# Groups of 8 samples by 64 d instead of 128 samples by 4 d: x stored straight from the gathered rows, and the sums over d taken inside a group

## What is computed

```python
e = stack([tbl_f[ids[:, f]] for f in range(32)], axis=1)        # B x 32 x 64
hidden = x = e
for i, (w, b) in enumerate([(w0, b0), (w1, b1)]):
    z = einsum('bhd,bfd->bhfd', hidden, x).reshape(B, -1, D)
    y = relu(einsum('bcd,oc->bod', z, w) + b[None, :, None])     # 128 channels o
    if i == 0: hidden, direct = y[:, :64], y[:, 64:]
    else:      direct = y
    finals.append(direct)
h = concatenate([concatenate(finals, 1).sum(-1), dense_ctx], 1)  # sum over d
h = relu(h @ W_top1 + b_top1); h = relu(h @ W_top2 + b_top2); y = h @ W_top3
```

## Time and profile before

| | us |
|---|---|
| three runs, median (lowest, highest) | 1093.7 (1091.5, 1093.88) |
| the profiled execution | 1092.62 |
| its span, first to last instruction | 1090.8 |
| TensorE busy | 1025.0 (94%) |
| VectorE busy | 944.4 (87%) |
| GpSimd busy | 915.5 (84%) |
| ScalarE busy | 734.9 (67%) |

### The profile page before, as it was taken

The page is one execution under the profiler, slowest core; times in us unless marked ns, Lnnn a source line. Parts: engine busy times, 40 slices in busy tenths (PEclk is TensorE's granted clock), DMA queues, the critical chain, the costliest instruction groups (busy, mean ns, idle before and its releaser), DMA issues.

```text
span 1090.8 us, 10701 instructions
## 1 busy us (share of the span) xinstructions
PE 1025.0 (94%) x3493; PEld 651.4 (60%) x3493; DVE 944.4 (87%) x623; ACT 734.9 (67%) x907; POOL 915.5 (84%) x300
## 2 busy tenths in 40 slices
PE   2059999999999999999999999999999999999999
PEld 1025556656666666666666666666666666666664
DVE  4059999999999999999999999999998989888982
ACT  1036666767777677777777777777777777777761
POOL 7526878779999999999999899997989888988890
PEclk9569999999999999999999999999999999999999
DMA  4278777687878787778877878787777877786730
GB/s 137 55 188 200 194 186 184 180 198 190 210 178 205 183 213 187 192 191 199 207 185 192 201 181 208 182 206 194 194 184 194 204 183 187 191 208 184 183 84 1
DMA packets 142074, 196.89 MB, mean 180 GB/s; under 512 B 15858, under 2 KB 57458, under 8 KB 141891
## 3 DMA queue, kind: packets, MB, share of 16 engines
q1 hardware_dynamic: 137922, 192.01, 70.3%
q0 software_dynamic: 4096, 4.20, 1.8%
HBM read 175.18 MB, written 20.97 MB: 180 GB/s over the span
## 4 chain that ended last, share of the span: by engine, by line
PE 86%; DVE 4%; issue 4%; DMA 3%; ACT 2%; SPq 1%; DVEq 0%; ACTq 0%
PE py L610 40%; PE py L626 15%; PE py L616 14%; PE py L617 14%; DVE zf L498 2%; ACT zh L362 2%; PE py L631 1%; DMA xs<-x_dram 1%; DMA x_dram<-xf 1%; DMA xs<-in_L_rec_w 1%; PE pt L592 1%; DVE zl L515 1%; PE py L675 0%; PE pzS L675 0%; DVE zf L459 0%
## 5 line engine op out<-in xcount | busy, mean ns | idle before, releaser
L303 POOL TENSOR_TENSOR zl<-zf,zh 128x2048 fp32r<-128x2048 f32 x168 | 772.3, 4610 | 116.2 <-ACT zh L362 114.2
L498 DVE TENSOR_TENSOR zf<-xs,hid 128x2048 f32<-128x2048 f32 x256 | 583.3, 2283 | 67.1 <-ACT hid L377 51.9
L610 PE MATMUL py<-zf,wf 128*128 128x512 f32 x1072 | 485.2, 596 | 6.5 <-DVE zf L498 6.5
L362 ACT ACTIVATE zh<-zf 128x2048 fp32r<-128x2048 f32 x186 | 354.9, 1908 | 44.5 <-DVE zf L498 41.1
L610 PEld LDWEIGHTS py<-zf,wf 128*128 128x128 f32 x1072 | 203.5, 190 | 214.2 <-issue 194.2
L616 PE MATMUL py<-zh,wh 128*128 128x512 f32 x744 | 293.6, 395 | 8.7 <-ACT zh L362 8.7
L617 PE MATMUL py<-zh,wl 128*128 128x512 f32 x744 | 292.1, 393 | 0.0
L626 PE MATMUL py<-zl,wh 128*128 128x512 f32 x744 | 233.8, 436 | 0.0
L498 DVE TENSOR_TENSOR zf<-xs,px 128x2048 f32<-128x2048 f32 x64 | 146.4, 2288 | 37.8 <-DMA xs<-x_dram 35.9
L626 PEld LDWEIGHTS py<-zl,wh 128*128 128x128 f32 x744 | 135.9, 189 | 59.2 <-issue 29.2
L293 POOL DMA_INDIRECT emb<-in_tbl,idx x128 | 143.1, 1118 | 29.9 <-issue 24.5
(11 more groups left out here) (71 smaller groups left out, 439.8 us busy)
## 6 DMA issues: line engine op xcount, KB each, us to landing
xs<-x_dram SPq DMA_DIRECT2D x640, 256.0 KB
x_dram<-xf SPq DMA_DIRECT2D x64, 320.0 KB
emb<-in_tbl,idx POOLq DMA_INDIRECT x128
xs<-in_L_rec_w SPq DMA_DIRECT2D x2, 512.0 KB
xs<-in_L_rec_w SPq DMA_DIRECT2D x1, 1024.0 KB
wt<-in_W_top SPq DMA_DIRECT2D x1, 512.0 KB
wt1b<-in_W_top SPq DMA_DIRECT2D x1, 256.0 KB
wt1a<-in_W_top SPq DMA_DIRECT2D x1, 128.0 KB
```

The lines of the kernel that those rows point to most:

```text
L303: pool.tensor_tensor(zl[:, q], zf[:, s], zh[:, q].bitcast(F32), ALU.subtract).then_inc(lo["P"], 1)
L362: act.activation(zh[:, q], zf[:, s], ACT.Copy).then_inc(hi, 1)
L498: dve.tensor_tensor(zf[:, slot(u)], left, right, ALU.mult).then_inc(mult, 1)
L610: mm = pe.matmul(y, wf[:, w, h], zf[:, s, h], start=first and h == 0, stop=ends and h == T - 1)
```

## The change

A group becomes NS = 8 samples by all 64 d. Then a gathered row (one sample, one field, 64 d, 256 B) is already a piece of a row of x, and:

- `stage_x`, `turn_x`, `copy_xf`, the tiles `stage`, `xf`, `pt` and their waits go. SyncE stores x straight from `emb`, in batches of fields as they are gathered (`store_batch`), in pieces of 256 B, five copies as before. `x_dram` is laid out by chunk, so a group's rows are 2048 B pieces at a step of 32 KB. Loads have the sizes they had.
- Chunk 0 is gathered and stored in batches of 12, 12, 6 and 2 fields. Later chunks go 3 or 2 fields a period, stored one period after the gather, in the same place of SyncE's order where `store_x` stood. `emb` holds two chunks instead of four; GpSimd waits for a chunk's stores before it gathers over it.
- A group holds whole sums over d: `add_1`, `add_2` and `sum_d` are replaced by one TENSOR_REDUCE a layer and group out of PSUM, 512 elements to 8 results (`sum_1`, `sum_2`).
- `py1` gets a second PSUM bank (the one of `pt`), so P(g+1) no longer waits for the readers of P(g), but for those of P(g-1). `sum_1(g)` stands behind the products of P(g+1) and its tail, not ahead of them.
- In the beginning xd(1) is loaded ahead of x0(1), xt(1) and xe(0).

```diff
-            def store_x(k):
-                sp.wait_ge(xf_ready, k + 1)
-                dst = x_dram[k, 0:1, :]
-                sp.dma_start(bass.AP(tensor=dst.tensor, offset=dst.offset, ap=[[N, F], [P, ND], [F * N, REPEATS], [1, P]]),
-                             view(xf, 0, [[0, REPEATS], [1, P]])).then_inc(x_stored, 16)
+            def store_batch(n):
+                c, f, m = BATCHES[n]
+                sp.wait_ge(gathered[n % BATCH_SEMS], gathered_count(n))
+                if m < REPEATS:
+                    for i in range(m):
+                        dst = x_dram[c, f + i:f + i + 1, :]
+                        sp.dma_start(bass.AP(tensor=dst.tensor, offset=dst.offset, ap=[[D, P], [F * P * D, REPEATS], [1, D]]),
+                                     view(emb, (c % 2 * F + f + i) * D, [[0, REPEATS], [1, D]])).then_inc(x_stored[c], 16)
+                else:
+                    for i in range(REPEATS):
+                        dst = x_dram[c, i * F + f:i * F + f + 1, :]
+                        sp.dma_start(bass.AP(tensor=dst.tensor, offset=dst.offset, ap=[[D, P], [P * D, m], [1, D]]),
+                                     emb[:, c % 2, f:f + m, :]).then_inc(x_stored[c], 16)
...
-                if g + 3 < G:
-                    store_x(g + 3)
+                if g >= 1 and batch_of(g - 1) is not None:
+                    store_batch(batch_of(g - 1))
...
+                if i == 0 and c >= 2:
+                    pool.wait_ge(x_stored[c - 2], 16 * STORES[c - 2])
+                if i == 0 and n >= BATCH_SEMS:
+                    pool.wait_ge(gathered[n % BATCH_SEMS], gathered_count(n - BATCH_SEMS))
...
                 high(("C", g))
                 if g >= 1:
                     finish_2(g - 1)
-                if g + 3 < G:
-                    copy_xf(g + 3)
                 high(("B", g))
...
+            def sum_1(k):
+                dve.wait_ge(dir1_ready, k + 1)
+                dve.tensor_reduce(zd[H:P, NS * k:NS * k + NS], py1[H:P, k % 2].rearrange("p (b d) -> p b d", d=D),
+                                  AX_X, ALU.add).then_inc(sum1_done, 1)
...
-                add_1(g)
                 if g + 1 < G:
                     products(("P", g + 1))
                     products_s(g + 1)
+                sum_1(g)
...
-                if name == "P" and g >= 1:
-                    pe.wait_ge(swapped, 3 * g)
-                    pe.wait_ge(acc1_done, g)
+                if name == "P" and g >= 2:
+                    pe.wait_ge(swapped, 3 * (g - 1))
+                    pe.wait_ge(sum1_done, g - 1)
...
-                if g + 3 < G:
-                    turn_x(g + 3)
```

More of the change, by code:

```diff
@@ L17 @@
 NC = B // P
[L18 to L21, removed]
+NS = 8
+N = NS * D
+G = B // NS
+GC = P // NS
 T = 4
@@ L47, in mode, with gathered_count, batch_of @@
     return "P"
[L52 to L57, removed]
+FIRST_BATCHES = [(0, 0, 12), (0, 12, 12), (0, 24, 6), (0, 30, 2)]
+PER_PERIOD = [[3] * 10 + [2], [2] * 16, [2] * 16]
+LATER_BATCHES = [(c, sum(PER_PERIOD[c - 1][:i]), n) for c in range(1, NC) for i, n in enumerate(PER_PERIOD[c - 1])]
+BATCHES = FIRST_BATCHES + LATER_BATCHES
+BATCH_SEMS = 4
+STORES = [sum(min(m, REPEATS) for b, _, m in BATCHES if b == c) for c in range(NC)]
+def gathered_count(n):
+    return 16 * sum(BATCHES[i][2] for i in range(n % BATCH_SEMS, n + 1, BATCH_SEMS))
+def batch_of(g):
+    return len(FIRST_BATCHES) + g if g < len(LATER_BATCHES) else None
 def period(g):
@@ L166, in dlrm_tower @@
         px0 = ps("px0", [P, N])
-        pt = ps("pt", [P, N])
         pzS = ps("pzS", [P, N])
[L169 to L174, removed]
+        banks = [py1[:, 0], py2[:, 0], py2[:, 1], hid[:, 0], hid[:, 1]]
+        top1 = [hid[:, 0], hid[:, 1], px0[:], py1[:, 0]]
+        top2 = [pzS[:], py1[:, 1]]
+        x_dram = nc.dram_tensor("x_dram", [NC, REPEATS * F, P * D], F32, kind="Internal")
         ids_in, consts_in, cin_in, top_in = sem("ids_in"), sem("consts_in"), sem("cin_in"), sem("top_in")
-        gathered = [sem("gathered%d" % c) for c in range(NC)]
+        gathered = [sem("gathered%d" % i) for i in range(BATCH_SEMS)]
+        x_stored = [sem("x_stored%d" % c) for c in range(NC)]
         cleared, w_doubled, w_turned = sem("cleared"), sem("w_doubled"), sem("w_turned")
         w_high, w_low, s_low, dense_turned = sem("w_high"), sem("w_low"), sem("s_low"), sem("dense_turned")
-        staged, turned, xf_ready, x_stored = sem("staged"), sem("turned"), sem("xf_ready"), sem("x_stored")
         x0_in, xt_in, xe_in = sem("x0_in"), sem("xt_in"), sem("xe_in")
@@ L261, in load_xe @@
                     sp.dma_start(xe[F * j:F * j + F], block_rows(k, j, T)).then_inc(xe_in, 16)
+            for n in range(len(FIRST_BATCHES)):
+                store_batch(n)
             sp.wait_ge(w_turned, 6)
-            store_x(0)
             load_x0(0)
@@ L290, in _, with gather @@
             pool.wait_ge(ids_in, 16)
-            def gather(c, f):
+            def gather(n, i):
+                c, first, m = BATCHES[n]
+                if i >= m:
+                    return
+                f = first + i
+                if i == 0 and c >= 2:
+                    pool.wait_ge(x_stored[c - 2], 16 * STORES[c - 2])
+                if i == 0 and n >= BATCH_SEMS:
+                    pool.wait_ge(gathered[n % BATCH_SEMS], gathered_count(n - BATCH_SEMS))
                 pool.indirect_dma_start(
-                    out=emb[:, f, c, :], out_offset=None, in_=tables[f],
+                    out=emb[:, c % 2, f, :], out_offset=None, in_=tables[f],
                     in_offset=bass.IndirectOffsetOnAxis(ap=idx[:, c, f:f + 1], axis=0),
-                ).then_inc(gathered[c], 16)
+                ).then_inc(gathered[n % BATCH_SEMS], 16)
             def low(u):
@@ L303, in low @@
                 pool.tensor_tensor(zl[:, q], zf[:, s], zh[:, q].bitcast(F32), ALU.subtract).then_inc(lo["P"], 1)
-            for f in range(F):
-                gather(0, f)
+            for n, (_, _, m) in enumerate(FIRST_BATCHES):
+                for i in range(m):
+                    gather(n, i)
             for g in range(G):
-                now = gathers(g)
+                n = batch_of(g)
                 low(("A", g))
-                for c, f in now[0:1]:
-                    gather(c, f)
+                if n is not None:
+                    gather(n, 0)
                 low(("C", g))
-                for c, f in now[1:2]:
-                    gather(c, f)
+                if n is not None:
+                    gather(n, 1)
                 low(("B", g))
-                for c, f in now[2:3]:
-                    gather(c, f)
+                if n is not None:
+                    gather(n, 2)
         @block.scalar
@@ L560, in _ @@
                 if g >= 1:
-                    add_2(g - 1)
+                    sum_2(g - 1)
                 low(("C", g))
                 products(("D", g))
[L565 to L571, removed]
+            sum_2(LAST)
         @block.tensor
@@ L586, in _ @@
             tr.then_inc(dense_turned, 1)
[L588 to L592, removed]
             def bank(u):
-                return py1[:] if u[0] == "P" else py2[:, u[1] % 2]
+                return (py1 if u[0] == "P" else py2)[:, u[1] % 2]
             def main(u):
@@ L630, in tail @@
                 pe.wait_ge(s_lo, k + 1)
-                pe.matmul(py1[:], wS[:], zS[:], start=False, stop=True).then_inc(y1_ready, 1)
+                pe.matmul(py1[:, k % 2], wS[:], zS[:], start=False, stop=True).then_inc(y1_ready, 1)
             def top_1_begin(m):
@@ L641, in _ @@
             pe.wait_ge(w_low, 3)
-            turn_x(0)
-            turn_x(1)
-            turn_x(2)
             main(("P", 0))
```

109 lines of the change are left out of this document (31 added, 78 removed).

## The result

The changed kernel takes 1102.4 us (median of 14 runs, 1097.5 to 1109.2) against 1093.7: the ratio is 1.009, with a 95% interval of 1.0073 to 1.0107. I had forecast 1085.5 and a range of 1079 to 1096. It became slower. The rival that names the cause (rival 4, the loads come in slower) had been given 0.05.

A forecast was written before the change was run, and what follows sets the result against it. TensorE, busy 94% of the span, was taken as the limit. Span 1090.8 less 7.3 (transposes), 3.8 (copy wait), 1.8 (chunk borders), plus 5.3 (later start) gave 1083.2, hence 1085.5 us forecast; range 1079 to 1096.

The forecast's parts named there:

- rival 4: Loads of 2048 B at a 32 KB step come in slower, DMA full at about 25% more; 1095 us and more; chance 0.05.
- the DMA queues take their new work hidden: Three fields a period cost 2.6 us of stores against 1.16; with 3.7 us of 16.2 free, 1.5 more is hidden.
- the one for rival 4: Sign of slower loads: growing waits of ScalarE for x0, or of VectorE for xd and xe.
- Transposes: 61 TensorE transposes in the periods go, 0.12 us each: 7.3 us gained.
- The high part of B behind the transposed copy: Periods 1, 3, 5, 7, 9: without ScalarE's copy it starts 2 us earlier, saving 0.78 us five times: 3.8 us.
- The chunk borders: VectorE's `sum_d` goes; 0.92 us lost at each of two borders is regained: 1.8 us.
- The reductions: On VectorE 127 additions become 127 PSUM reductions at 0.70 us each, costing nothing since VectorE stays under TensorE.
- Rival 1: Reductions take 1.06 us whatever they read, so VectorE would bound periods 0 to 42; 1088 to 1090 us; chance 0.12.
- The small stores: Twice as many DMA pieces of 256 B, taken at 22 ns each, bounds 19 and 29.
- Rival 2: Small stores are slow, a 256 B packet costing more than a 512 B one; 1104 to 1115 us at 40 ns; chance 0.13.
- The beginning as a whole: Storing chunk 0 delays the first load to about 56.5 us, 5.3 later; then 8.1 to P(0), 15.1 more to A(0).
- The sum: All terms together: 1090.8 - 7.3 - 3.8 - 1.8 + 5.3 = 1083.2 us of span.

The follow-up runs named there:

- the run with 36 KB: The changed kernel with each row of x_dram 4 KB longer, so rows lie at a step of 36 KB instead of 32 KB: 1082.9 us, ratio 0.9908.

## Why the prediction was wrong

**The step that failed** is the sentence that the DMA queues take their new work hidden ("DMA is 0.77 busy, so 3.7 us of 16.2 are free"), together with rival 4's "DMA would go from 0.77 to full at about 25% more; below that nothing". Both weigh throughput, and the sum has no term for how late a load lands. DMA never was full: from 100 to 300 us 0.83 in the changed kernel and 0.87 in the faster one with 36 KB, from 300 to 600 us 0.83 in both. What counted was how late one load lands, in a circle of waits. In the stretch from P(12) to P(44) x0's mean way went from 5.5 to 7.4 us, and the period came out at 15.81 instead of 15.36. Against the run with 36 KB that is 14.5 us there, and 6.4 more from P(0) to P(12): the loss of some 20 us. Of the signs that I had named, the one for rival 4 came (waits of ScalarE for x0 that grow, 24.6 to 209.3 us); its mechanism, DMA near full, did not.

The circle was in the trace of before. ScalarE's copy already waited for x0 there, 21 times in the periods. By the turns of the changed kernel and 0.3 us for `stage_x`, the mean turn of before is about 8.8 + 5.5 = 14.3 us of 15.47, an estimate: 1.2 us of slack, less than the 1.8 us that x0 then became later. I saw the wait on x0 while reading and set it aside, since TensorE was idle nowhere.

What lengthened x0's way was the new layout. I wrote "Loads have the sizes they had" and went on as if they had the time they had. The median went from 5.5 to 6.6 us with the step alone and to 7.0 and over with the stores beside it. The nearest rule is in the Trainium skill, DMA: Bandwidth & Descriptors, section Latency and other measured facts: for copies of 16 KiB a partition it gives 207 GB/s at a row pitch of 512 KiB, 164 at 2 MiB and 103 at 4 MiB, and nothing below 512 KiB. It would have let 32 KB pass. Here 32 KB is slow (1101.5 to 1105.3 us), while 64 and 128 KB are not (1083.6 and 1082.8).

**The steps that held.** The others, read in the run with 36 KB where nothing else is named, since no late load covers them there:
- Transposes: a period of 15.36 where it was 15.47, 0.12 each.
- The high part of B behind the transposed copy: early pairs at 31.42, forecast 31.4, before 32.40.
- The chunk borders: from P(12) on no pair in that run is longer than 30.72.
- The reductions: 0.695 and 0.684 us, forecast 0.70. Rival 1 falls. In the changed kernel itself:

```profile
L526 DVE TENSOR_REDUCE zsum<-py 128x8 f32<-128x512 f32 x64 | 44.1, 689 | 38.1 <-ACT py L404 37.9
...
L521 DVE TENSOR_REDUCE zd<-py 64x8 f32<-64x512 f32 x64 | 44.5, 695 | 2.0
```

- The small stores: in the beginning a piece of 256 B takes a mean of 18 ns, beside the loads 20, where I took 22 (512 B: 29 to 30). The first load goes out at 55.71 against 56.5. Rival 2 falls: small stores are not dear as it had it. The rule of the Trainium skill that it leaned on (DMA: Bandwidth & Descriptors, Specifications: no full rate below 512 B) agrees in so far as a byte costs 1.2 to 1.3 times as much as in pieces of 512 B. The stores have a part in the loss all the same: without the later ones 14 of the 19.5 us come back, beside loads with the 32 KB step and not beside others.
- The beginning as a whole came out right partly by luck: the load went out 0.8 us sooner than forecast, and P(0) followed 9.3 us behind it instead of 8.1, so that A(0) at 79.85 meets the forecast of 79.7.
- The sum: 1083.2 us of span; the run with 36 KB has 1081.5. Its terms were right to within about 1 us each, and what was missing is a term for the landing of the loads.

## What to carry to other kernels

When data get a new layout in DRAM, the loads from it are a changed operation even if their sizes stay: price their landing, and try another step early, since it costs one constant (here 256 B more were enough). Before calling a transfer hidden, follow the circle that it lies on: what it waits for, what stands behind its reader in that engine's order, and how that leads back. Compare its mean turn with the period; the busy share does not tell (0.83 in the slow kernel, 0.83 to 0.87 in the fast one). An engine beside a full one that waits a little in many periods says that there is such a circle, not that its slack is used up: with 36 KB ScalarE waits for x0 62 times in the periods, and the circle still has 1 us to spare.

## What the runs showed of the hardware that I had not expected

Loads of 2048 B pieces from rows exactly 32 KB apart land later: with no stores about, x0's median is 6.3 to 6.6 us after its issue, against 5.6 to 5.8 with 36 KB, 64 KB, 32 KB + 256 B, 128 KB or rows close together. Beside the small stores it is 6.9 to 7.1 with single loads up to 10.3 (groups 12 to 43), against 5.7 to 6.3 and at most 7.8 with the other steps. The mean time of a 2048 B packet hardly differs (137 ns against 134), but the slowest twentieth starts at 328 ns instead of 187, so the busy share does not show it. A tensor twice as large and a shift by 4 KB made no difference. Why 32 KB is bad and its multiples are not stays open: no run here tells it. A store of 256 B pieces took 18 to 20 ns a piece, about what the gathers of 256 B rows had shown (19), not as much as one of 512 B (29 to 30).
